# Reordering one head's step on four engines, and splitting a product, in the first attention of a four-stage kernel

## The chip, the cores and the metric

The kernel runs on one core of a Trainium2 chip. The core has a matrix engine (TensorE, PE in the rows; PEld is its weight load), a vector engine (VectorE, DVE), a scalar engine (ScalarE, ACT), GpSimd (POOL) and SyncE (SP), which here only starts transfers. The metric is the device time of one launch in microseconds. Of the kernel before there are three runs: 1880.74, 1884.63 and 1884.85 us, median 1884.63 us.

## The reference, cut to what matters

The input x is 8 x 512 x 128. It passes four blocks, each of the form `x = layernorm(x + block(x))`. The change is in the first one, an attention with 16 heads of 8 channels in which each score also has two terms that depend on the clipped distance of query and key:

```
Q, K, V = heads(x @ Wq.T + bq), heads(x @ Wk.T + bk), heads(x @ Wv.T + bv)      # 8 batches x 16 heads, 512 x 8
rel_pos = clip(k - q + 64, 0, 127);  p2c_pos = clip(q - k + 64, 0, 127)
scores  = Q @ K.T * scale
c2p     = take_along(Q @ pos_key.T * scale, rel_pos)
p2c     = take_along(K @ pos_query.T * scale, p2c_pos).T
probs   = softmax(scores + c2p + p2c)
ctx     = probs @ V;   out = ctx @ Wo.T + bo
```

The other blocks are a gated feed-forward layer, a second attention of 16 heads, and a ternary feed-forward layer. Everything is in float32.

## The kernel before, in words

The 8 x 16 = 128 heads of the first attention (`attention(0)`, where `rel` is true) are worked off one after the other. One head is one *step*; each engine has its own function for a step (`shifted_tensor_step`, `shifted_vector_step`, `shifted_scalar_step`, `sync_step`), and these functions write the order of the engine's instructions out by hand. Four steps are unrolled ahead of a loop, the loop holds 8 steps, and the rest follows it. The engines meet only through semaphores. In a step of head h:

- The 512 x 512 scores are four tiles of 128 queries. **S** (`score_tile`, L821, L823, L827) makes a tile in a PSUM bank, S0 to S3 for the tiles 6 to 9 ahead of the head's first. Its last matmul (L827) writes one spare block into `bank[4]`, which all tiles share, so it waits until VectorE has used the spare block of the tile before (`fixed`).
- **M** (`mix`, L934) on VectorE copies that spare block into the tile under a mask, **F** (`finish`, L946) adds the band of distance terms, and **X** (`row_max`, L954) takes the negated row maximum. M and F of a step work on the tiles that S made; X on the tile one earlier (X0 to X3: 5 to 8 ahead). F needs the band, and X needs F of its tile.
- **E** (`exp_tile`, L1044) on ScalarE exponentiates, E0 to E3 for the tiles 4 to 7 ahead. E3 therefore follows X2, and it is the last tile of head h+1.
- **T** (`turn`, L842) transposes one column block k of the head's own probabilities by four matmuls, and **CT** (`copy_turned`, L1051) on ScalarE copies it to SBUF. T0 of the next step waits for E3 and CT3 of this one; T2 waits for CT1, T1 for the correction's copy (CO, L761), and T3 for KO.
- **W** (`weigh`, L855) multiplies the probabilities of the *previous* four heads (a group, `GROUP` = 4) with their values: step j of a group adds column block j % 4 of all four heads, in four float32 matmuls of 32 output rows each, one per head, side by side in the array. After the last of the four steps ScalarE copies the group's result out (**GO**, `group_out`, L1057), and SyncE stores it (L671) and then loads new values (L673).
- **K** (`key_side`, L741) makes a distance table of the keys for the head 7 ahead, in a bank that CT0 must have emptied; VectorE copies it out (**KO**, L755). SyncE writes it to `shear_a` (L634), waits until it has landed, and reads it back skewed (L640, `a_sheared`). **C** (`correction`, L748 and L749) of the head 5 ahead needs this; ScalarE copies it out (CO, L761), and SyncE writes it to `shear_b` (L646) and reads the skewed band (L652).
- SyncE also loads the operands of the head 8 ahead (`head_load`, L608, L609), and once in a group a table and offsets (L621 to L629). Its queue is in order, so each `hold` (a wait) stops all that is behind it.

Of the kernel before, what the change touches and what calls it, by code (L numbers as in the profile page):

```python
# [21 lines left out]
B, T, C = 8, 512, 128  # L22
# [23 lines left out]
GROUP = 4  # L46
# [4 lines left out]
CORR_AHEAD, KEY_AHEAD, LOAD_AHEAD = 5, 7, 8  # L51
# [13 lines left out]
def build(nc, t):  # L65

    top = ExitStack()
    with top:
# [430 lines left out]
        def attention(layer):  # L499
# [175 lines left out]
            def sync_step(sp, i, j, left, weighed=True):  # L675

                n = unroll * i + j
                if rel:
                    if left >= CORR_AHEAD + 1:
                        shear_a_write(sp, Head(i, j + CORR_AHEAD + 1))  # L680
                    if left >= LOAD_AHEAD:
                        hold(sp, score_mm, 4 * (n + 1))
                        head_load(sp, Head(i, j + LOAD_AHEAD))
# [3 lines left out]
                    if left >= CORR_AHEAD - 2:  # L687
                        shear_b_read(sp, Head(i, j + CORR_AHEAD - 2))
                    if j % GROUP == GROUP - 1 and left >= LOAD_AHEAD + GROUP:
                        tab_load(sp, Head(i, j + LOAD_AHEAD + 1))  # L690
# [98 lines left out]
            def program(block, before, after):  # L789
# [79 lines left out]
                def shifted_tensor_step(pe, i, j, left, weighed=True):  # L869
# [4 lines left out]
                    turn(pe, own, 1)  # L874
                    if left >= KEY_AHEAD:
                        pe.wait_ge(copied, BASE + 4 * own.n + 1)
                        key_side(pe, Head(i, j + KEY_AHEAD), key_bank)
                    if weighed:
                        weigh(pe, Head(i, j - j % GROUP - GROUP), j % GROUP, slice(0, T))
                    turn(pe, own, 2)  # L880
                    score_ahead_of(pe, i, j, left, 2)
                    turn(pe, own, 3)
                    score_ahead_of(pe, i, j, left, 3)
# [84 lines left out]
                def _(v):  # L968
# [26 lines left out]
                    def shifted_vector_step(i, j, left, weighed=True):  # L995
                        mix_ahead_of(i, j, left, 0)
                        max_ahead_of(i, j, left, 0)
                        mix_ahead_of(i, j, left, 1)
                        finish_ahead_of(i, j, left, 0)
                        finish_ahead_of(i, j, left, 1)  # L1000
                        max_ahead_of(i, j, left, 1)
                        if left >= KEY_AHEAD:
                            key_out(v, Head(i, j + KEY_AHEAD), key_bank)
                        max_ahead_of(i, j, left, 2)
                        mix_ahead_of(i, j, left, 2)
# [54 lines left out]
                def _(act):  # L1060
# [8 lines left out]
                    def shifted_scalar_step(i, j, left, weighed=True):  # L1069
                        own = Head(i, j)  # L1070
                        copy_turned(act, own, 0)
                        exp_ahead_of(i, j, left, 0)
# [3 lines left out]
                        copy_turned(act, own, 2)  # L1076
                        exp_ahead_of(i, j, left, 3)
                        copy_turned(act, own, 3)
                        if weighed and j % GROUP == GROUP - 1:
                            group_out(act, Head(i, j - j % GROUP - GROUP))  # L1080
# [1041 lines left out]
```

## Time and profile before

| | |
|---|---|
| profiled execution | 1880.74 us, span 1879.0 us |
| median of three runs | 1884.63 us |
| PE busy | 1699.8 us, 90% |
| DVE busy | 1468.3 us, 78% |
| ACT busy | 1448.4 us, 77% |
| transfers | 404.45 MB, 69.3% of 16 engines' time |

One execution is profiled, so times inside the program are compared with 1879.0 us and not with the median. Busy shares are means over four blocks with different limits; the first attention takes about the stretch from 180 to 830 us, in which PE, DVE and ACT are all near nine or ten tenths busy. PE's matmuls overlap in the pipeline, so its busy share is not the share of its peak. What follows is read from start to start of instructions in this stretch.

### The profile page before, as it was taken

The page shows a single profiled execution, that of the slowest core. Times are in us where ns is not written, and L with a number is a line of the kernel's source. Part 1 is how long each engine was busy: PE and PEld are TensorE (multiplying, and loading weights), DVE is VectorE, ACT ScalarE, POOL GpSimd, SP SyncE. Part 2 cuts the span into 40 slices and gives each one's busy share as a digit, 9 for nine tenths or more (in the row PEclk, how much of TensorE's full clock was granted, in tenths as well). Part 3 has the DMA queues.
Part 4 walks back from the last instruction along what each step waited for, and adds up shares of the span by engine and source line. Part 5 has one row for each costly group of instructions (what it writes and reads, how often), then busy time and mean ns, then how long its engine had stood idle before and what let it go on. Part 6 is the DMA issues. An engine that isn't in the chain of part 4 may idle for free.

```text
span 1879.0 us, 44062 instructions
## 1 busy us (share of the span) xinstructions
PE 1699.8 (90%) x11694; PEld 1033.3 (55%) x11694; DVE 1468.3 (78%) x3533; ACT 1448.4 (77%) x2573; POOL 80.2 (4%) x102
## 2 busy tenths in 40 slices
PE   5369999999999999878758999999999989999998
PEld 2146666666666666545535666666666544455453
DVE  5659999999999999859887999999999873443332
ACT  4449999998999999859888999999999972322222
POOL 0000000000000000015410000000000000000000
PEclk9669999999999999989879999999999999999999
DMA  6778999998999999766998777777777751010000
GB/s 195 273 245 274 300 292 307 298 297 278 288 289 295 297 287 301 234 190 231 344 333 241 220 221 217 223 219 217 222 221 213 224 155 40 28 39 22 22 6 12
DMA packets 414360, 404.45 MB, mean 215 GB/s; under 512 B 36969, under 2 KB 334561, under 8 KB 414177
## 3 DMA queue, kind: packets, MB, share of 16 engines
q1 hardware_dynamic: 414305, 403.80, 69.3%
q8 instruction: 24, 0.39, 0.1%
q14 instruction: 31, 0.25, 0.0%
HBM read 226.89 MB, written 176.30 MB: 215 GB/s over the span
## 4 chain that ended last, share of the span: by engine, by line
PE 54%; DMA 14%; SPq 9%; issue 7%; DVE 7%; ACT 6%; DVEq 0%; POOL 0%; ACTq 0%; POOLq 0%
PE bank L842 15%; PE bank L1934 12%; PE bank L855 8%; DMA a_band<-shear_e 5%; PE bank L821 5%; DMA shear_a<-a_keyside 4%; PE bank L748 3%; DMA a_sheared<-shear_a 2%; DVE a_negmax L954 2%; PE bank L823 2%; ACT a_probt L1051 2%; PE bank L1926 1%; PE bank L1927 1%; PE bank L827 1%; PE bank L1955 1%
## 5 line engine op out<-in xcount | busy, mean ns | idle before, releaser
L1044 ACT ACTIVATE a_prob<-bank,a_negmax 128x512 f32<-128x512 f32 x1024 | 702.6, 741 | 27.4 <-DVE a_negmax L954 25.8
L954 DVE TENSOR_REDUCE a_negmax<-bank 128x1 f32<-128x512 f32 x1024 | 695.1, 679 | 0.2 <-issue 0.2
L1051 ACT COPY a_probt<-bank 128x512 f32<-128x512 f32 x1024 | 599.4, 633 | 28.0 <-PE bank L842 23.5
L842 PE MATMUL bank<-ident,a_prob 128*128 128x128 f32 x4096 | 602.6, 281 | 13.1 <-ACT a_probt L1051 9.7
L842 PEld LDWEIGHTS bank<-ident,a_prob 128*128 128x128 f32 x4096 | 446.4, 142 | 170.9 <-ACT a_probt L1051 117.3
L946 DVE TENSOR_TENSOR bank<-bank,a_band 128x128 f32<-128x128 f32 (+3 forms) x1024 | 339.1, 343 | 71.9 <-DMA a_band<-shear_e 24.4
L821 PE MATMUL bank<-a_stks 74*128 74x192 bf16 (+7 forms) x1024 | 324.7, 317 | 29.7 <-ACT a_prob L1044 26.0
L855 PE MATMUL bank<-a_probt,a_vs 128*32 128x512 f32 x2048 | 274.8, 611 | 0.8 <-ACT a_probt L1051 0.4
L823 PE MATMUL bank<-a_stks 74*128 74x320 bf16 (+5 forms) x768 | 201.3, 262 | 0.0
L821 PEld LDWEIGHTS bank<-a_stks 74*128 74x128 bf16 (+1 forms) x1024 | 100.5, 98 | 163.8 <-ACT a_prob L1044 143.6
L934 DVE COPY_PREDICATED bank<-a_mask,bank 128x128 f32<-128x128 uint32 (+1 forms) x512 | 140.2, 274 | 20.1 <-PE bank L827 18.6
L748 PE MATMUL bank<-ident,a_sheared 128*128 128x128 f32 x512 | 110.3, 293 | 33.2 <-DMA a_sheared<-shear_a 25.8
L2000 DVE TENSOR_TENSOR d_drop<-bank,d_s 128x128 f32<-128x128 f32 x32 | 7.1, 283 | 170.4 <-PE bank L1955 170.4
L827 PE MATMUL bank<-a_stks 74*128 74x128 bf16 (+1 forms) x512 | 112.0, 219 | 6.2 <-DVE bank L934 5.8
L761 ACT COPY a_corr<-bank 128x512 f32<-128x512 f32 x128 | 76.2, 595 | 51.8 <-PE bank L749 38.6
L1934 PE MATMUL bank<-d_ha,d_h1T 128*128 128x512 f32 x256 | 112.3, 592 | 0.0
L1934 PE MATMUL bank<-d_hb,d_h2T 128*128 128x512 f32 x256 | 111.2, 592 | 0.0
L755 DVE COPY a_keyside<-bank 128x512 f32<-128x512 f32 x128 | 86.7, 678 | 19.8 <-PE bank L741 19.8
L748 PEld LDWEIGHTS bank<-ident,a_sheared 128*128 128x128 f32 x512 | 74.8, 146 | 46.5 <-issue 25.1
L749 PE MATMUL bank<-a_tabs,a_stks 65*128 65x128 bf16 x512 | 98.6, 226 | 0.0
L1985 ACT ACTIVATE d_hb<-bank,d_fs 128x512 f32<-128x512 f32 x32 | 22.0, 688 | 90.6 <-PE bank L1934 90.6
L827 PEld LDWEIGHTS bank<-a_stks 74*128 74x128 bf16 x512 | 49.3, 96 | 73.3 <-DVE bank L934 47.9
(179 smaller groups left out, 1597.5 us busy)
## 6 DMA issues: line engine op xcount, KB each, us to landing
a_band<-shear_b SPq DMA_DIRECT2D x128, 512.0 KB, 5.2
shear_a<-a_keyside SPq DMA_DIRECT2D x128, 256.0 KB, 4.1
a_sheared<-shear_a SPq DMA_DIRECT2D x128, 256.0 KB, 4.1
shear_b<-a_corr SPq DMA_DIRECT2D x128, 256.0 KB, 3.4
shear_e<-a_corr SPq DMA_DIRECT2D x128, 256.0 KB, 2.3
a_band<-shear_e SPq DMA_DIRECT2D x128, 256.0 KB, 3.3
a_stks<-stack SPq DMA_DIRECT2D x256, 96.0 KB, 2.5
a_stks<-stack SPq DMA_DIRECT2D x384, 48.0 KB, 2.4
```

Of the source, the lines that this page charges most:

```text
L748: pe.matmul(corr_bank[:, q], sheared[h.slot % 4][:, q], ident[:, :], is_transpose=True, start=True, stop=False)
L821: last = pe.matmul(score[:, 0:c], k[:, qlo, q], k[:, keys, 0:c], start=True, stop=True)
L823: last = pe.matmul(score[:, c:T], k[:, qhi, q], k[:, keys, c:T], start=True, stop=True)
L827: last = pe.matmul(other[:, 0:e - a], k[:, qhi, q], k[:, keys, a:e], start=True, stop=True)
L842: last = pe.transpose(turned_bank[k][:, n * 128:(n + 1) * 128], prob[h.slot % 2][:, n, k * 128:(k + 1) * 128], ident[:, :])
L855: part = pe.matmul(cbank[32 * j:32 * j + VW, cols], vs[g][:, at:at + VW], probt[h.slot + j][:, k, cols], start=(k == 0), stop=(k == NT - 1 ...
L934: v.copy_predicated(score[:, a:e], mask[:, 0:e - a], other[:, 0:e - a]).then_inc(fixed, 1)
L946: v.tensor_tensor(score[:, a:e], score[:, a:e], band[h.slot % bands][:, n, w:w + e - a], ALU.add).then_inc(added, 1)
L954: v.tensor_reduce(negmax[h.slot % 2][:, n:n + 1], score[:, :], AX.X, ALU.max, negate=True).then_inc(maxed, 1)
L1044: nc.scalar.activation(prob[h.slot % 2][:, n, :], score[:, :], ACT.Exp, bias=negmax[h.slot % 2][:, n:n + 1]).then_inc(exped, 1)
L1051: nc.scalar.copy(probt[h.slot][:, k, :], turned_bank[k][:, :]).then_inc(copied, 1)
L1934: last = pe.matmul(dst[:, :], w[:, k, 128 * m:128 * m + 128], src[:, k, :], start=(k == 0), stop=(k == KH - 1))
```

## The change

On PE, W moves from behind K to ahead of it, S2 moves from behind T2 to ahead of it, and in three of four steps W is cut into two halves of 256 columns, the second behind T2. On VectorE, each F comes after an X, so that M and F of one tile no longer stand side by side. On ScalarE, E0 moves ahead of CT0, and GO moves from behind CT3 to ahead of E3. On SyncE the operand load moves behind the two `shear_b` transfers, and waits for the row maxima of the head in place of its scores.

```diff
@@ sync_step
-                    if left >= LOAD_AHEAD:
-                        hold(sp, score_mm, 4 * (n + 1))
-                        head_load(sp, Head(i, j + LOAD_AHEAD))
                     if left >= CORR_AHEAD - 1:
                         hold(sp, added, 4 * (n + 1))
                         shear_b_write(sp, Head(i, j + CORR_AHEAD - 1))
                     if left >= CORR_AHEAD - 2:
                         shear_b_read(sp, Head(i, j + CORR_AHEAD - 2))
+                    if left >= LOAD_AHEAD:
+                        hold(sp, maxed, 4 * (n + 1))
+                        head_load(sp, Head(i, j + LOAD_AHEAD))
@@ shifted_tensor_step
                     turn(pe, own, 1)
+                    if weighed:
+                        weigh(pe, Head(i, j - j % GROUP - GROUP), j % GROUP, slice(0, T // 2 if j % GROUP else T))
                     if left >= KEY_AHEAD:
                         pe.wait_ge(copied, BASE + 4 * own.n + 1)
                         key_side(pe, Head(i, j + KEY_AHEAD), key_bank)
-                    if weighed:
-                        weigh(pe, Head(i, j - j % GROUP - GROUP), j % GROUP, slice(0, T))
+                    score_ahead_of(pe, i, j, left, 2)
                     turn(pe, own, 2)
-                    score_ahead_of(pe, i, j, left, 2)
+                    if weighed and j % GROUP:
+                        weigh(pe, Head(i, j - j % GROUP - GROUP), j % GROUP, slice(T // 2, T))
+                    score_ahead_of(pe, i, j, left, 3)
                     turn(pe, own, 3)
-                    score_ahead_of(pe, i, j, left, 3)
@@ shifted_vector_step
                         max_ahead_of(i, j, left, 0)
+                        finish_ahead_of(i, j, left, 0)
                         mix_ahead_of(i, j, left, 1)
-                        finish_ahead_of(i, j, left, 0)
+                        max_ahead_of(i, j, left, 1)
                         finish_ahead_of(i, j, left, 1)
-                        max_ahead_of(i, j, left, 1)
                         if left >= KEY_AHEAD:
                             key_out(v, Head(i, j + KEY_AHEAD), key_bank)
+                        mix_ahead_of(i, j, left, 2)
                         max_ahead_of(i, j, left, 2)
-                        mix_ahead_of(i, j, left, 2)
                         finish_ahead_of(i, j, left, 2)
@@ shifted_scalar_step
+                        exp_ahead_of(i, j, left, 0)
                         copy_turned(act, own, 0)
-                        exp_ahead_of(i, j, left, 0)
                         copy_turned(act, own, 1)
                         exp_ahead_of(i, j, left, 1)
                         exp_ahead_of(i, j, left, 2)
                         copy_turned(act, own, 2)
+                        if weighed and j % GROUP == GROUP - 1:
+                            group_out(act, Head(i, j - j % GROUP - GROUP))
                         exp_ahead_of(i, j, left, 3)
                         copy_turned(act, own, 3)
-                        if weighed and j % GROUP == GROUP - 1:
-                            group_out(act, Head(i, j - j % GROUP - GROUP))
```

PE before, in one step of a loop turn: T1 (L842), K (L741), the four matmuls of W (L855), T2, and S2 (L821 to L827).

```order
L842 MATMUL bank<-ident,a_prob_52 128x128 x4
L739 ISA
L740 ISA
L741 MATMUL bank<-a_stks,a_tabs 128x512
L855 MATMUL bank<-a_probt_57,a_vs_62 32x512
L855 MATMUL bank<-a_probt_58,a_vs_62 32x512
L855 MATMUL bank<-a_probt_59,a_vs_62 32x512
L855 MATMUL bank<-a_probt_60,a_vs_62 32x512
L842 MATMUL bank<-ident,a_prob_52 128x128 x4
L820 ISA
L821 MATMUL bank<-a_stks 128x192
L823 MATMUL bank<-a_stks 128x320
```

PE now, the same place: T1, the first half of W, K, S2, T2, and the start of the second half.

```order
L842 MATMUL bank<-ident,a_prob_52 128x128 x4
L855 MATMUL bank<-a_probt_57,a_vs_62 32x256
L855 MATMUL bank<-a_probt_58,a_vs_62 32x256
L855 MATMUL bank<-a_probt_59,a_vs_62 32x256
L855 MATMUL bank<-a_probt_60,a_vs_62 32x256
L739 ISA
L740 ISA
L741 MATMUL bank<-a_stks,a_tabs 128x512
L820 ISA
L821 MATMUL bank<-a_stks 128x192
L823 MATMUL bank<-a_stks 128x320
L825 REGISTER_ALU
```

W stood between K and T2 in one piece; now K stands behind W, and S2 and T2 stand between the halves.

VectorE before, from KO (L755) over X2 (L954), M2 (L934), F2 (L946), M3 and X3 to F3.

```order
L755 COPY a_keyside_73<-bank 128x512
L954 TENSOR_REDUCE a_negmax_63<-bank 128x1
L931 ISA
L934 COPY_PREDICATED bank<-a_mask,bank 128x128
L946 TENSOR_TENSOR bank<-bank,a_band_71 128x192
L931 REGISTER_ALU
L934 COPY_PREDICATED bank<-a_mask,bank 128x128
L953 REGISTER_ALU
L954 TENSOR_REDUCE a_negmax_64<-bank 128x1
L946 TENSOR_TENSOR bank<-bank,a_band_71 128x256
```

VectorE now, the same place (its lines are two further down in the file).

```order
L755 COPY a_keyside_73<-bank 128x512
L933 ISA
L936 COPY_PREDICATED bank<-a_mask,bank 128x128
L956 TENSOR_REDUCE a_negmax_63<-bank 128x1
L948 TENSOR_TENSOR bank<-bank,a_band_71 128x192
L933 REGISTER_ALU
L936 COPY_PREDICATED bank<-a_mask,bank 128x128
L955 REGISTER_ALU
L956 TENSOR_REDUCE a_negmax_64<-bank 128x1
L948 TENSOR_TENSOR bank<-bank,a_band_71 128x256
```

X2 has moved in between M2 and F2; KO stays ahead of both.

## Rows read from the trace of the kernel before

**Rows 1.** The page's costliest groups: line, engine, op | busy, mean ns | idle before.

```profile
L842 PE MATMUL bank<-ident,a_prob 128*128 128x128 f32 x4096 | 602.6, 281 | 13.1 <-ACT a_probt L1051 9.7
L855 PE MATMUL bank<-a_probt,a_vs 128*32 128x512 f32 x2048 | 274.8, 611 | 0.8 <-ACT a_probt L1051 0.4
```

**Rows 2.** Busy us of each engine from 200 to 700 us; then clock, DMA share, GB/s.

```profile
200.00:700.00 500.00, 488.65 (x4087) 316.10 (x4085) 476.01 (x1208) 470.37 (x860) 0.00 (x0) 1.00 0.93 293
```

**Rows 3.** Groups by line from 200 to 700 us: C's transposes and their waits.

```profile
L748 PE MATMUL bank<-ident,a_sheared 128*128 128x128 f32 x372 | 77.2, 285 | 9.5 <-DMA a_sheared<-shear_a 7.0 <-ACT a_probt L1051 2.3
```

**Rows 4.** Timeline of DVE: start us, length us, engine, line; one step.

```profile
501.01 0.28 DVE L934 COPY_PREDICATED bank<-a_mask,bank 128x128 f32<-128x128 uint32 x1
...
501.81 0.22 DVE L934 COPY_PREDICATED bank<-a_mask,bank 128x64 f32<-128x64 uint32 x1
501.94 0.69 DVE L946 TENSOR_TENSOR bank<-bank,a_band 128x256 f32<-128x256 f32 x2
...
503.13 0.68 DVE L755 COPY a_keyside<-bank 128x512 f32<-128x512 f32 x1
503.73 0.68 DVE L954 TENSOR_REDUCE a_negmax<-bank 128x1 f32<-128x512 f32 x1
504.33 0.28 DVE L934 COPY_PREDICATED bank<-a_mask,bank 128x128 f32<-128x128 uint32 x1
504.73 0.37 DVE L946 TENSOR_TENSOR bank<-bank,a_band 128x192 f32<-128x192 f32 x1
505.06 0.30 DVE L934 COPY_PREDICATED bank<-a_mask,bank 128x128 f32<-128x128 uint32 x1
505.26 0.68 DVE L954 TENSOR_REDUCE a_negmax<-bank 128x1 f32<-128x512 f32 x1
...
506.19 0.29 DVE L934 COPY_PREDICATED bank<-a_mask,bank 128x128 f32<-128x128 uint32 x1
```

**Rows 5.** Timeline of PE, one step, first matmul of each block.

```profile
500.61 0.63 PE L842 MATMUL bank<-ident,a_prob 128*128 128x128 f32 x4
...
501.07 0.38 PE L821 MATMUL bank<-a_stks 74*128 74x512 bf16 x1
...
501.44 0.65 PE L842 MATMUL bank<-ident,a_prob 128*128 128x128 f32 x4
501.93 0.38 PE L741 MATMUL bank<-a_stks,a_tabs 65*128 65x512 bf16 x1
502.24 1.06 PE L855 MATMUL bank<-a_probt,a_vs 128*32 128x512 f32 x8
503.23 0.66 PE L842 MATMUL bank<-ident,a_prob 128*128 128x128 f32 x4
503.73 0.25 PE L821 MATMUL bank<-a_stks 74*128 74x192 bf16 x1
...
504.00 0.61 PE L842 MATMUL bank<-ident,a_prob 128*128 128x128 f32 x4
...
504.77 0.30 PE L748 MATMUL bank<-ident,a_sheared 128*128 128x128 f32 x1
...
505.78 0.63 PE L842 MATMUL bank<-ident,a_prob 128*128 128x128 f32 x4
```

**Rows 6.** Timeline of PEld, the weight load behind W.

```profile
503.23 0.42 PEld L842 LDWEIGHTS bank<-ident,a_prob 128*128 128x128 f32 x4 [0.84 <-ACT a_probt L1051]
```

**Rows 7.** Timeline of ACT: E3, CT3, and GO of the next step.

```profile
504.44 0.71 ACT L1044 ACTIVATE a_prob<-bank,a_negmax 128x512 f32<-128x512 f32 x1
505.03 0.60 ACT L1051 COPY a_probt<-bank 128x512 f32<-128x512 f32 x1
...
510.68 0.61 ACT L1057 COPY a_outs<-bank 128x512 f32<-128x512 f32 x1
```

**Rows 8.** Timeline of SP's queue: the skewed read, and the group's store.

```profile
510.50 0.35 SPq L640 DMA_DIRECT2D a_sheared<-shear_a  x1
511.55 0.38 SPq L671 DMA_DIRECT2D heads_out<-a_outs  x1
```

## The prediction

> **What bounds the kernel now.** I read the busy shares first, then the timelines of one undisturbed step engine by engine, then the groups by line, for who waits. From 200 to 700 us PE, DVE and ACT are busy for 489, 476 and 470 of 500 us at the full clock (1.00, that is 2.4 GHz), and the transfers take 0.93 of the 16 DMA engines' time [rows 2]. So everything is nearly full, and the busy shares name no bound. C's four transposes per head number 372, so 93 heads pass in these 500 us, 5.38 us each [rows 3]. An undisturbed step is shorter: VectorE starts M0 at 501.01 and the next M0 at 506.19, 5.18 us, and no row in between shows an idle gap [rows 4]. PE's step from T0 to T0 is 5.17 us, but S1 to T1 takes 0.37 us where S2 to T3 takes 0.27 for more columns: 0.10 is a wait for VectorE [rows 5]. VectorE sets an undisturbed step. The other 0.20 us per head are disturbances; about half of it is C, which waits for its skewed read: 9.5 us in 500 [rows 3], 0.10 per head.
>
> The change touches some 30 groups of four heads. That is the unit of the sum: 0.1 us per group is 3 us.
>
> **VectorE.** M2 to F2 takes 0.40 us, and F2 to M3 0.33, where M3 to X3 takes 0.20 [rows 4]: F2 needs M2, which is 0.28 long, so it starts 0.12 behind M2's end. With X2 in between, M2 takes 0.20, and F2 0.27 (F0 and F1 together take 0.59: 1.19 from F0 to KO less one X of 0.60 [rows 4]). That saves 0.26. Against it, X1 now stands only one M1 (0.13) behind the F0 that it needs. A shorter F is 0.37 long; with the same 0.12 that is 0.49 at least against 0.33 + 0.13 = 0.46, and for F0's 256 columns I take 0.07 of new wait; X3 has 0.02 of the same kind. With the rest kept VectorE's own step is 5.18 - 0.26 + 0.09, about 5.02.
>
> **PE: what W costs in two halves.** One matmul of 512 columns is recorded with 0.611 us, one of 128 with 0.281 [rows 1], both float32: 0.86 ns per column. W's x8 are two ranks of four side by side, so 2 x 512 x 0.86 = 0.88 of its 0.99 us [rows 5] are columns and 0.11 is fixed. Half a W is then 0.44 + 0.11 = 0.55. The bounds of this unseen block are 0.50 (half of 0.99, all of it columns) and 0.99 (none of it); I take 0.55, since the column rate comes from rows. Ahead of W stands a gap: K is 0.13 longer than S2's first matmul for 320 more columns, so its 512 columns take 0.21, but W starts 0.31 behind it [rows 5]: 0.10. The load behind W starts with T2 itself at 503.23, after PEld idled for 0.84 us [rows 6]: weights are not brought in while W runs, at either edge.
>
> With T = 0.46 (T0 to S1), S = 0.27, K = 0.21, S3 and T3 together 0.73 and C with S0 1.01 (C to T0) [rows 5], and the gap of 0.10 ahead of each W, a step with halves, counted from T0, has S1 at 0.46, T1 0.73, W 1.29, K 1.84, S2 2.05, T2 2.32, the second half 2.88, S3 3.43, T3 3.70, C 4.16, and the next T0 at 5.17. A step with a whole W has K at 2.28 and PE would be through at 4.96. PE is therefore the new limit of the three split steps, at 5.17, against VectorE's 5.02: what VectorE gains is hidden behind it.
>
> **A wait that comes in with the whole W.** In one step of four K stands behind a whole W: it starts at 2.28, not at 1.32 as now (501.93 - 500.61). It is 0.38 long, so KO starts at about 2.72; M2 stands behind KO at 3.32, and X2 at 3.52. Behind that stand others: X2 ends and E3 starts 0.71 behind X2's start (503.73 to 504.44 [rows 4, 7]), CT3 0.59 later, and CT3 is 0.60 long [rows 7], with some 0.05 to PE. T0 of the next step needs both: 3.52 + 0.71 + 0.59 + 0.65 = 5.47. In the kernel before the same chain has 1 us to spare.
>
> **ScalarE.** E0 ahead of CT0 uses the time in which ScalarE waits for T0; K and T2 need CT0 and CT1, and in the new order reach them 0.5 us later than now, so this costs nothing as long as K stays behind W. GO ahead of E3 has a price: the second half of W starts at 2.88 and drains by 2.88 + 0.55 + 0.07 (1.06 less 0.99 [rows 5]) = 3.50; GO at 3.53, E3 half a us behind it at 4.03, CT3 4.62, next T0 5.27. It occurs once in a group.
>
> Sum of a group: 5.47 + 5.27 + 2 x 5.17 = 21.08 against 4 x 5.18 = 20.72, so +0.36, times 30: +11 us.
>
> **SyncE and the transfers.** The chain behind C's waits starts at GO: it starts at 510.68 and is 0.61 long, the store is issued at 511.55 [rows 7, 8], and the shear_a write, its landing and the skewed read for a C two steps later stand behind the store. GO comes at 3.53 instead of 4.90 (510.68 less 505.78), but the skewed read of its own step is issued only at 510.50 and each issue takes about half a us, so the store can move from 511.55 to about 511.05 at most. Besides, PE's and ScalarE's longer step leaves the transfers 0.36 us more per group. C's waits are 9.5 x 30 x 21.5 / 500, about 12 us over the stage (21.5 is four heads of 5.38). I take three quarters of it as gone, -9 us; the bounds are 0 and -12. The operand load moved behind the shear_b transfers costs nothing: it fills the time until shear_a has landed, and its new condition, X2 of the step before, is older than the write ahead of it. In the group's last step the shear_b write may now stand and wait for CO for a few tenths, in front of the loads; that is in the 0 to -12.
>
> Net: +11 - 9 = +2 us. From the profiled 1880.74 that is 1883; from the median, 1884.63, it is 1887, and I name 1886.
>
> **Rule of the Trainium skill against the rows.** The rows show no weight load under a running W [rows 6]. The Trainium skill, TensorE: Matmul & The Clock Gate, section Part 2, says that the engine's reorder window pulls weight loads ahead of matmuls in flight when row groups do not conflict or the background buffer is free. By that rule neither edge of W would cost anything, and halving it would be nearly free; that is the first rival below. The trace speaks against it.
>
> **The rivals.**
> - *The edges of W are hidden once it stands between other blocks.* For it: K and S2 bring bfloat16 weights, unlike T2, whose load is the one that the rows show late. Against it: the 0.10 between K and W is such an edge, and it is not hidden. Without gaps (0.10 ahead and 0.11 fixed, per block) a split step is 4.75 on PE, so VectorE limits it to 5.02; the whole-W chain is 5.47 - 0.21 = 5.26. Group 5.26 + 3 x 5.02 = 20.32, -0.40, times 30 = -12, with C's waits -9 more: 1864.
> - *The halves cost more than their columns.* PE is then the bound through six halves per group. Each 0.01 us on a half is 0.06 per group, 1.8 us in all. At 0.65 (0.10 over mine, well inside the bound of 0.99) a split step is 5.37, and the sum +2 + 18 = +20: 1905. For it: each half loads its four weights anew. Against it: no row shows a fixed part above 0.11. It decides from 0.57 on, where the loss passes 0.3%.
> - *The transfers bound it.* 0.93 x 5.38 = 5.00 us of the DMA engines per head; nothing below 5.0 can be had, and near it landing times grow. It takes away a faster PE's gain and leaves 1885.
>
> That the order does not change is excluded: the four functions write it out.
>
> **Numbers.** Forecast (no change that shows) 0.38, with the transfer case in it; its own range is 1879 to 1890. Hidden edges, and cases between, 0.28; costly halves, or C's waits unrelieved with the +11 in full (1896), 0.34. About 0.3%, 5.7 us, is what a measurement tells from no change. Faster 0.29, same 0.37, slower 0.34. The range reaches most of the way to both rivals: 1866 to 1904.
>
> **What would show it.** In the new profile: VectorE without the 0.40 behind M2, but with idle time again; half a W at 0.55 from its start to the next block; in one step of four KO released by K and the next T0 late by 0.3; GO about 3.5 us behind T0; the wait at L748 well under 9.5 us in the same stretch. I am wrong if the undisturbed group is under 20.5 us, or if a half takes 0.60 or more.

## The result, and the profile after

The changed kernel takes 1936.22 us (median of four runs, 1933.13 to 1944.24) against 1884.68 us for the kernel before on the same chip: ratio 1.0285, 95% interval 1.0251 to 1.032. It is slower by 52 us. I had forecast 1886 us and a range that ended at 1904. The profiled execution took 1944.98 us, with a span of 1943.2.

Busy time of each engine from 200 to 700 us after, with the clock, the DMA share and GB/s at the end. It answers to [rows 2].

```profile
200.00:700.00 500.00, 461.63 (x4243) 307.87 (x4245) 430.52 (x1103) 432.57 (x783) 0.00 (x0) 0.97 0.88 268
```

All three engines have lost 27 to 46 us of work in the same 500 us, and the transfers have dropped from 0.93 to 0.88. So neither an engine nor the transfers became the bound: everybody waits. The clock is no longer fully granted either (0.97). The groups by line of the same stretch (busy us, mean ns, then idle us ahead and who ended it) say who is waited for; the first answers to [rows 3].

```profile
L748 PE MATMUL bank<-ident,a_sheared 128*128 128x128 f32 x340 | 71.3, 287 | 0.0
...
L755 DVE COPY a_keyside<-bank 128x512 f32<-128x512 f32 x85 | 58.4, 687 | 47.4 <-PE bank L741 47.4
...
L741 PE MATMUL bank<-a_stks,a_tabs 65*128 65x512 bf16 x84 | 32.6, 388 | 30.1 <-DMA a_stks<-stack 20.3 <-issue 7.7 <-ACT a_probt L1053 1.9
```

KO (L755) numbers 85, so a head takes 5.88 us instead of 5.38. C's wait is gone, from 9.5 us to nothing, as forecast in number; whether for the reason that I gave is taken up behind the experiments. In its place K (L741) waits for its operands, a wait that the kernel before does not have. The list of waits shows two more places (us in total, times, longest); the first row is K's weight load, the other two are SyncE's own queue.

```profile
PEld bank L741 <- issue: 43.6, 28, 2.8
...
SPq L598 <- ACT a_corr L761: 85.4, 54, 3.4
SPq L598 <- DMA shear_a<-a_keyside: 31.9, 22, 2.3
```

SyncE's waits of the kernel before, in the same view:

```profile
SPq L598 <- DMA shear_a<-a_keyside: 68.8, 63, 3.8
...
SPq L598 <- ACT a_corr L761: 1.6, 1, 1.6
```

It waited for `shear_a` to land, 18 times for GO (12.0 us, none of it left now), and once for CO. Now it stands 54 times in the `hold` for CO, with the operand load queued behind. One such place in full: PE and ACT first (start us, length, engine, line, idle time ahead in brackets), then SyncE's queue.

```profile
502.14 0.64 PE L855 MATMUL bank<-a_probt,a_vs 128*32 128x256 f32 x8
504.77 0.39 PE L741 MATMUL bank<-a_stks,a_tabs 65*128 65x512 bf16 x1 [1.99 <-DMA a_stks<-stack]
...
505.29 0.61 PE L842 MATMUL bank<-ident,a_prob 128*128 128x128 f32 x4
...
507.00 1.06 PE L842 MATMUL bank<-ident,a_prob 128*128 128x128 f32 x4
...
509.47 0.59 ACT L761 COPY a_corr<-bank 128x512 f32<-128x512 f32 x1 [0.78 <-PE bank L749]
```

```profile
497.35 0.37 SPq L646 DMA_DIRECT2D shear_b<-a_corr  x1
497.84 0.58 SPq L652 DMA_DIRECT2D a_band<-shear_b  x1
498.84 0.34 SPq L608 DMA_DIRECT2D a_stks<-stack  x1
499.37 0.35 SPq L609 DMA_DIRECT2D a_stks<-stack  x1
...
510.14 0.37 SPq L646 DMA_DIRECT2D shear_b<-a_corr  x1
```

K is ready to start behind the half W, at about 502.8, and starts at 504.77. The load that it needs was issued at 499.37, 2.0 us behind the `shear_b` write, and behind the 512 KB band read, with only its own first part (L608) between. As PE works in order, T, C and CO come late with it, and the next `shear_b` write is only issued at 510.14. The stop costs more than its 2 us: this step takes 8.79 us from T0 (500.87) to T0 (509.66). Two windows of 6 us around it (same columns as above):

```profile
500.00:506.00 6.00, 3.83 (x39) 2.47 (x40) 3.75 (x10) 4.07 (x9) 0.00 (x0) 1.00 1.00 315
506.00:512.00 6.00, 6.00 (x48) 3.94 (x41) 4.33 (x13) 4.32 (x8) 0.00 (x0) 0.72 0.62 182
```

After PE has been idle for 2 us the granted clock falls to 0.72 in the next window; from 507 to 509 us it is 0.50, the 1.2 GHz level. There T's four matmuls take 1.06 us instead of 0.61.

### The profile page after: what moved, and what is told of

It reads as the page before. It is cut to its first block, busy times and chain, and to the rows that moved or that the text cites. A ratio compares the mean times of both kernels' runs of the same rounds, so it can differ in the third digit from the quotient of the medians.

```text
span 1943.2 us, 45550 instructions
## 1 busy us (share of the span) xinstructions
PE 1721.4 (89%) x12438; PEld 1057.7 (54%) x12438; DVE 1463.4 (75%) x3533; ACT 1453.5 (75%) x2573; POOL 80.1 (4%) x102
## 4 chain that ended last, share of the span: by engine, by line
PE 43%; SPq 16%; issue 13%; DMA 12%; DVE 8%; ACT 7%; DVEq 0%; POOL 0%; ACTq 0%; POOLq 0%
PE bank L1936 11%; PE bank L842 10%; PE bank L855 6%; DMA a_band<-shear_e 6%; DMA a_stks<-stack 4%; PE bank L821 4%; DVE a_negmax L956 3%; ACT a_probt L1053 3%; ACT a_prob L1046 2%; PE bank L823 2%; PE bank L1928 1%; PE bank L1929 1%; DVE bank L948 1%; PE bank L741 1%; PE bank L748 1%
## 5 line engine op out<-in xcount | busy, mean ns | idle before, releaser
L1053 ACT COPY a_probt<-bank 128x512 f32<-128x512 f32 x1024 | 584.9, 624 | 71.7 <-PE bank L842 70.8
L842 PE MATMUL bank<-ident,a_prob 128*128 128x128 f32 x4096 | 603.8, 281 | 21.8 <-ACT a_probt L1053 15.5
L842 PEld LDWEIGHTS bank<-ident,a_prob 128*128 128x128 f32 x4096 | 451.8, 143 | 89.9 <-issue 51.3
L948 DVE TENSOR_TENSOR bank<-bank,a_band 128x128 f32<-128x128 f32 (+3 forms) x1024 | 350.4, 342 | 58.8 <-DMA a_band<-shear_e 29.0
L821 PE MATMUL bank<-a_stks 74*128 74x192 bf16 (+7 forms) x1024 | 328.1, 321 | 33.9 <-ACT a_prob L1046 30.6
L855 PE MATMUL bank<-a_probt,a_vs 128*32 128x256 f32 (+1 forms) x2792 | 298.1, 501 | 0.4 <-ACT a_probt L1053 0.4
L821 PEld LDWEIGHTS bank<-a_stks 74*128 74x128 bf16 (+1 forms) x1024 | 100.6, 98 | 218.7 <-ACT a_prob L1046 176.8
L755 DVE COPY a_keyside<-bank 128x512 f32<-128x512 f32 x128 | 87.9, 687 | 83.0 <-PE bank L741 82.8
L748 PE MATMUL bank<-ident,a_sheared 128*128 128x128 f32 x512 | 109.7, 292 | 25.3 <-DMA a_sheared<-shear_a 20.3
L827 PE MATMUL bank<-a_stks 74*128 74x128 bf16 (+1 forms) x512 | 111.2, 217 | 5.9 <-DVE bank L936 4.8
L741 PE MATMUL bank<-a_stks,a_tabs 65*128 65x512 bf16 x128 | 51.3, 400 | 58.1 <-DMA a_stks<-stack 25.9
L855 PEld LDWEIGHTS bank<-a_probt,a_vs 128*32 128x32 f32 x2792 | 56.3, 109 | 68.2 <-issue 68.0
```

The costliest lines, as they stand in the source:

```text
L748: pe.matmul(corr_bank[:, q], sheared[h.slot % 4][:, q], ident[:, :], is_transpose=True, start=True, stop=False)
L821: last = pe.matmul(score[:, 0:c], k[:, qlo, q], k[:, keys, 0:c], start=True, stop=True)
L827: last = pe.matmul(other[:, 0:e - a], k[:, qhi, q], k[:, keys, a:e], start=True, stop=True)
L842: last = pe.transpose(turned_bank[k][:, n * 128:(n + 1) * 128], prob[h.slot % 2][:, n, k * 128:(k + 1) * 128], ident[:, :])
L855: part = pe.matmul(cbank[32 * j:32 * j + VW, cols], vs[g][:, at:at + VW], probt[h.slot + j][:, k, cols], start=(k == 0), stop=(k == NT - 1 ...
L948: v.tensor_tensor(score[:, a:e], score[:, a:e], band[h.slot % bands][:, n, w:w + e - a], ALU.add).then_inc(added, 1)
```

## The experiments

Ratios are to the kernel before on the same chip, with the 95% interval. All waits are sums over 200 to 700 us. The notation "e1 +" means that a kernel starts from e1, which is the changed kernel with SyncE's old order.

**Which engine's order costs the time?** First SyncE: once taken back, once put alone into the kernel before.

```diff
@@ sync_step (e1: the changed kernel; e2 is the kernel before with the reverse edit)
+                    if left >= LOAD_AHEAD:
+                        hold(sp, score_mm, 4 * (n + 1))
+                        head_load(sp, Head(i, j + LOAD_AHEAD))
                     ...shear_b_write, shear_b_read
-                    if left >= LOAD_AHEAD:
-                        hold(sp, maxed, 4 * (n + 1))
-                        head_load(sp, Head(i, j + LOAD_AHEAD))
```

> The changed kernel with SyncE's old order (operand load first, released by the scores). Theory A: the load of the head 8 ahead now stands behind the shear_b write, which waits for the correction's copy, so it lands too late for K one step later (67 waits for that copy, 105 us, and PE's K waiting 20 us for a load by name, 84 us in all, from 200 to 700 us); with the old order K waits for no load and the time is 1875 to 1892 us. Theory B: the orders on PE, VectorE and ScalarE (halved W, K behind W) are the loss; then it stays at 1920 or more. An even split would read about 1910.

> The kernel before with SyncE's new order alone. Theory A: most of the loss is here, 1920 to 1945 us, with PE waiting at L741 for the operand load. Theory B: no change, 1880 to 1890. A rival within A: in the old PE order K comes early in the step (1.3 us behind T0 instead of 1.8 or 2.3), so a late load hurts more here than in the changed kernel, over 1945.

Measured: e1 0.9967 (0.9942 to 0.9993), e2 1.0428 (1.0384 to 1.0472). e2's median is 1973 us, over the 1920 to 1945 of theory A, as its rival with the earlier K had it. (The 67 waits and 105 us for CO in the first expectation belong to a stretch that reaches beyond 700 us; up to there they are the 54 and 85.4 above.) The whole loss is SyncE's, and it needs nothing of the other three edits; the three together save some 0.3%. K's waits in e1, then in e2:

```profile
DVE a_keyside L755 <- PE bank L741: 14.8, 46, 0.5
PEld bank L741 <- issue: 14.2, 23, 0.8
```

```profile
PEld bank L741 <- issue: 36.6, 21, 3.5
...
PE bank L741 <- DMA a_stks<-stack: 29.1, 11, 3.3
```

The 14.2 us of e1 come once in four steps (x23), with no transfer late: K's weights stand behind the whole W. Only what exceeds it I count as a load that is late. The profile names no releaser for these waits, so this is inferred from how they come and go with the load's place: they are 14.2 again in e3 and e13. It makes 29 us in the changed kernel, which with the 28 us of the PE row (20.3 and 7.7) makes 57. KO's wait says the same: 47.4 against 14.8.

**Is it the place of the load, or its new condition?** e3 has the new condition in the old place.

```diff
@@ sync_step (e1 +)
-                        hold(sp, score_mm, 4 * (n + 1))
+                        hold(sp, maxed, 4 * (n + 1))
```

> The changed kernel with the operand load back in its old place, but with the new condition (row maxima instead of scores). Theory A says the place is what costs, not the condition: within 0.5% of the kernel with SyncE's old order. If the condition costs, it lies with the changed kernel at about 1935.

Measured 0.9977 (0.9957 to 0.9997), and K waits for no load. It is the place.

**Which place?** Three other ones. A `shear_a` write opens SyncE's step, `shear_b` write and read follow, the skewed read of `shear_a` closes it.

```diff
@@ sync_step: order of the transfers
 before, e1     shear_a write, LOAD, shear_b write, band read, shear_a read
 after          shear_a write, shear_b write, band read, LOAD, shear_a read
+e5             shear_a write, shear_b write, LOAD, band read, shear_a read
+e12            shear_a write, shear_b write, band read, shear_a read, LOAD
+e13            LOAD, shear_a write, shear_b write, band read, shear_a read
```

> The changed kernel with the operand load between the shear_b write and the shear_b read: still behind the wait for the correction's copy, but one issue (about 0.5 us) and one wait earlier. If what costs is the wait for the copy ahead of the load, most of the loss stays: ratio to the kernel before 1.018 to 1.03 (changed kernel 1.0285). If it is the amount of transfers put ahead (a 512 KB band read among them), it falls to 1.00 to 1.012.

> The changed kernel with the operand load still further back, behind the skewed read of shear_a, which waits until the write of shear_a has landed (3.8 us). Loss theory: load, K, C, the correction's copy and the shear_b write that waits for it form a loop over two steps, in which every us ahead of the load adds 0.5 us per step. The load is issued 1 to 2 us later, so 0.5 to 1 us per step over 124 steps, 60 to 120 us on top of the changed kernel: ratio 1.06 to 1.095. If the loss came from the shear_b transfers being early, and not from the load being late, it stays near 1.03.

> SyncE's old order, but with the operand load at the head of the step, ahead of the shear_a write; the changed orders elsewhere. Theory: with the load ahead of the shear_b write K waits for no load any more, so an earlier load gains nothing: 0.997 as with the old order. If the shear_a write, its landing and the skewed read are what limits a disturbed step, a later shear_a write (by two issues, 1 us) shows as a loss, 1.003 to 1.01.

Measured: e5 1.0005 (0.9985 to 1.0025), e12 1.013 (1.01 to 1.0159), e13 0.9975 (0.996 to 0.9991). e5 also stands behind the wait for CO and costs nearly nothing. e12 is a miss: the load is issued later than in the changed kernel and yet only about half as much is lost. How late the load is issued does not by itself set the price, so my theory at that point fell. What differs is the time that the second load (L609) takes to land. For the kernels before, after, e5 and e12, in this order (us, minimum, median, maximum), and last for e14, which comes below:

```profile
DMA to landing us min/median/max: 1.8/3.1/6.0
```

```profile
DMA to landing us min/median/max: 3.0/4.3/5.7
```

```profile
DMA to landing us min/median/max: 2.1/3.8/5.1
```

```profile
DMA to landing us min/median/max: 2.0/2.9/4.1
```

```profile
DMA to landing us min/median/max: 2.6/3.8/5.1
```

**Wait for CO ahead, 512 KB ahead, or both?** e14 and e15 move the band read to the front; e16 leaves the new order as it is and fetches half of the band, e17 does this under the old order. In e16 and e17 half of each band row keeps old values, so the correction is computed from partly old numbers.

```diff
@@ sync_step: order of the transfers
+e14            shear_a write, band read, LOAD, shear_b write, shear_a read
+e15            shear_a write, band read, shear_b write, LOAD, shear_a read
@@ shear_b_read (e16: the changed kernel, e17: e1)
-                [[PITCH_B - 1, 128], [1, NT * wide]]
+                [[PITCH_B - 1, 128], [1, NT * wide // 2]]
```

> The changed kernel with SyncE's order band read, operand load, shear_b write: the load is directly behind the 512 KB read, as in the change, but no longer behind the write that waits for CO. Theory A (the load is late only when its issue, which stands behind CO, and its landing behind the 512 KB read add up past K's turn): it is issued some 2 us earlier, so a longer landing (4.0 to 4.6 us for the second load, 4.3 in the change) costs nothing; ratio 0.994 to 1.004, K waits for no load. Rival C (the 512 KB read directly ahead is enough by itself): 1.01 to 1.03 and K waits for loads 15 times or more in 500 us. Rival B (only the place behind CO counts): 0.997, like SyncE's old order, so it does not part from A here.

> The changed kernel with SyncE's order band read, shear_b write, operand load: against the change only the band read moves, from between write and load to ahead of the write, so the load stands behind the wait for CO as before, 0.5 us of issuing earlier, and behind 256 KB more recent transfers instead of 512. Theory A: landing of the second load 3.3 to 3.9 us (4.3 in the change), its issue 0.5 us earlier, margin 0.9 to 1.5 us larger; ratio 1.000 to 1.008, K's waits for the load under 20 us in 500. Rival B (the place behind CO is the price): 1.02 to 1.03, waits of 50 us or more. Rival C: 0.997 to 1.003.

> The changed kernel with SyncE's new order untouched; the band read fetches the first half of each row alone in the looped steps (256 KB instead of 512 KB; the other half of the band holds old values, so the scores' correction is computed from old numbers). Theory A: the load is issued at the same place behind CO, but lands behind 256 KB: second load 3.2 to 3.8 us instead of 4.3; ratio to the kernel before 0.990 to 1.004, K's waits for loads under 20 us in 500. Rival B (place behind CO): 1.015 to 1.03. To be read against the same halving under SyncE's old order.

> The same halving of the band read (256 KB of 512, the correction is computed from partly old numbers) with SyncE's old order and the changed orders of the three engines. 0.985 to 0.998: what 256 KB less a head give where no load is late. Theory A: within 0.5 per cent of the halved read under the new order. Rival B: 1.5 per cent or more faster than that. If transfers bounded this kernel, 15 per cent fewer bytes would bring it under 0.95.

Measured: e14 1.0482 (1.0453 to 1.0511), e15 1.0414 (1.039 to 1.0439). Both expectations failed, and neither kernel tests what it was made for: moved to the front, the band read meets its own write. SyncE's waits and a piece of its queue in e14:

```profile
SPq L598 <- DMA shear_b<-a_corr: 142.1, 60, 3.5
```

```profile
504.93 0.32 SPq L652 DMA_DIRECT2D a_band<-shear_b  x1
...
506.33 0.35 SPq L609 DMA_DIRECT2D a_stks<-stack  x1
506.87 0.39 SPq L646 DMA_DIRECT2D shear_b<-a_corr  x1
...
511.33 0.32 SPq L652 DMA_DIRECT2D a_band<-shear_b  x1
```

The band read of 511.33 waits for the write of 506.87 to land; in every order but these two the wait for CO of the following step lay between the two and hid it. SyncE's queue is now itself the loop that sets the step, 6.4 us long here. I had overlooked this wait when I wrote what to expect. One thing can still be read from e14: behind the 512 KB read, but ahead of the write, the second load lands after 3.8 us at the median, as it does in e5 behind the write alone. Behind both, in the changed kernel, it takes 4.3.

e16 and e17 do decide: e16 0.9988 (0.9975 to 1.0), e17 0.9945 (0.9921 to 0.997). With 256 KB less in front of it, the load in its bad place costs 0.4%, not 3.2% (1.0285 against 0.9967). SyncE's waits in e16, K's wait for the load, and the landing of L609:

```profile
SPq L598 <- ACT a_corr L762: 68.1, 59, 1.6
```

```profile
PE bank L742 <- DMA a_stks<-stack: 0.3, 1, 0.3
```

```profile
DMA to landing us min/median/max: 2.3/3.2/3.6
```

SyncE still waits for CO in 59 places, so the load is issued just as late; it lands 1.1 us sooner at the median and 2.1 us sooner at worst, and K no longer waits. The table puts this together for an undisturbed step. The write (L646) starts about 0.6 us behind T0 (0.7 in e2), L609 so much later as the second column says, and K of the next step is due 7.1 us behind T0 (5.21 + 1.85, and some hundredths; 6.5 in e2, which has PE's old order, 5.17 + 1.32). What is left for the landing is the third column. The fifth counts the landings that took longer than that.

| | L609 behind L646 | left for the landing | landing, median and longest | landings over what is left | K waits for loads | ratio |
|---|---|---|---|---|---|---|
| e16 | 1.94 | 4.6 | 3.2, 3.6 | 0 of 92 | 1 | 0.9988 |
| e5 | 1.36 | 5.1 | 3.8, 5.1 | 0 of 92 | 2 | 1.0005 |
| e12 | 3.39 | 3.1 | 2.9, 4.1 | 14 of 90 | 22 | 1.013 |
| after | 1.93 | 4.6 | 4.3, 5.7 | 30 of 84 | 57 | 1.0285 |
| e2 | 1.94 | 3.9 | 4.0, 5.7 | 45 of 81 | 62 | 1.0428 |

(Medians over 200 to 700 us; K's waits are PE's for the load and for issue at L741 plus its weight load's for issue, less the 14.2 of e1, or the 7.2 of the kernel before in e2.) In e16 and after, the same time is left, and only the landing differs: this pair shows that the late landing is what costs. In e12 the load has the least time left and still less is lost than in the changed kernel: half as many of its landings come too late. The count moves with the time left (with 0.1 us less it is 22 and 36 for e12 and after), the order of the five kernels does not.

e16 does not show that it is the place of the read alone that makes the landing long, since it also moves fewer bytes in all (a DMA share of 0.82 against 0.88). Four kernels with the same orders on the engines part the two: under SyncE's old order the median landing is 3.2 us with the whole read (e1) and 2.6 with half of it (e17), under the new order 4.3 (after) and 3.2 (e16). So 256 KB less per head shorten the landing by 0.6 us even where the load stands ahead of the read, and the place behind the two `shear_b` transfers adds 1.1 us with the whole read and 0.6 with half of it.

**What each other edit does.** PE's order alone, VectorE's alone, both without ScalarE's; SyncE's order is the old one in all three.

```diff
@@ the kernel before, with these functions taken from the changed kernel
+e4             shifted_tensor_step
+e9             shifted_vector_step
+e10            shifted_tensor_step, shifted_vector_step
```

> The kernel before with PE's new order alone (W ahead of K, halves, S2 ahead of T2). By the sum of the prediction PE's split steps take 5.17 us and the step with a whole W 5.47, on VectorE's old 5.18: theory A gives 1885 to 1900 us. Theory B gives 1910 or more.

> The kernel before with VectorE's new order alone. VectorE's own work falls to 5.02 us a step, so by that alone it is the fastest, ratio 0.985 or less. But M2 now stands ahead of X2, and in PE's old order S2, which M2 waits for, comes only behind K, W and T2, 3.1 us behind T0: S2's last matmul 3.3, M2 3.6, X2 3.8, E3 4.5, CT3 5.1, next T0 5.75. The chain theory says slower: undisturbed steps of about 5.7 us, ratio 1.04 to 1.07.

> The kernel before with the new orders on PE and VectorE, ScalarE and SyncE as before. PE's order alone gave 1.0137 (steps of 5.53 and 6.0 us). If the orders on PE and VectorE belong together and ScalarE's is a side matter, steps are 5.2 and 5.5 to 5.7, and the ratio lies with SyncE's old order alone (0.9967), 0.995 to 1.000. If ScalarE's E0 ahead of CT0 is needed, it stays above 1.005.

Measured: e4 1.0137 (1.0092 to 1.0183), e9 1.037 (1.0343 to 1.0397, just under what was expected), e10 1.0016 (0.9999 to 1.0034, just over the 0.995 to 1.000 expected). e4 is a miss: 1917 us where the sum of the prediction gave 1885 to 1900. The longest waits of e4, then of e9 (27.4 and 8.6 us in the kernel before):

```profile
PEld bank L827 <- DVE bank L936: 67.2, 177, 1.1
```

```profile
DVE bank L934 <- PE bank L827: 80.7, 83, 1.2
```

Each order alone waits for the other engine, through the spare block that all score tiles share. Only as a pair do they come out even; with ScalarE's they give the 0.3% of e1; e10 and e1 differ by no more than the edge of their intervals.

Then the three choices inside the new orders: K ahead of the whole W (e6), GO behind CT3 as before (e7), the whole W in every step (e8).

```diff
@@ shifted_tensor_step (e1 +, e6)
-                    if weighed:
-                        weigh(pe, ..., slice(0, T // 2 if j % GROUP else T))
+                    if weighed and j % GROUP:
+                        weigh(pe, ..., slice(0, T // 2))
                         key_side(pe, Head(i, j + KEY_AHEAD), key_bank)
+                    if weighed and j % GROUP == 0:
+                        weigh(pe, ..., slice(0, T))
@@ shifted_scalar_step (e1 +, e7)
-                        group_out ahead of exp_ahead_of(i, j, left, 3)
+                        group_out behind copy_turned(act, own, 3)
@@ shifted_tensor_step (e1 +, e8)
-                        weigh(pe, ..., slice(0, T // 2 if j % GROUP else T))
+                        weigh(pe, ..., slice(0, T))
                     ...
-                    if weighed and j % GROUP:
-                        weigh(pe, ..., slice(T // 2, T))
```

> SyncE's old order, the changed orders elsewhere, and K ahead of the whole W in the one step of four that has it. With SyncE's old order undisturbed steps take 5.21 us with halves and 5.77 with a whole W (group 21.42). If KO behind K behind the whole W makes the 5.77, this step falls to about 5.2 and the group to 20.85, 0.57 less: some 17 us, ratio to before about 0.988. If it is the W itself on PE, the step stays at 5.6 or more, and the ratio at 0.996. Transfers near their limit could give part of it back: 0.992.

> SyncE's old order, the changed orders elsewhere, but the group's copy (GO) behind CT3 as in the kernel before. The prediction held that the earlier GO relieves C's wait for its skewed read by up to 12 us in the stage: then this is slower than SyncE's old order alone (0.9967) by 0.3 to 0.6%, 1.000 to 1.003, and SyncE waits for GO at the store again. If the longer step on PE gave the relief, it stays at 0.997.

> SyncE's old order, the changed orders elsewhere, but W whole in every step, ahead of K. If the chain K, KO, X2, E3, CT3 behind a whole W sets a step at 5.77, all four take it: group 23.1 against 21.42, +1.65, times 30 is +50 us, ratio 1.022 (less where disturbed steps hide it: 1.012 and up). If PE's work per step rules, two blocks less per step make it faster than 0.9967.

Measured: e6 0.9984 (0.9958 to 1.0009), e7 0.9985 (0.9966 to 1.0005), e8 1.0075 (1.005 to 1.01). e6 (expected 0.988) and e8 (expected 1.012 to 1.022) are misses: both were reckoned from a whole-W step of 5.77 us and three of 5.21, but e1's group is one of 5.53 (whole W), one of 5.46 (GO) and two of 5.21. In e6 it takes 5.61: KO now comes early, but M2 stands idle for 0.50 us until PE has made S2's spare block, which the whole W ahead of S2 delays as much as it delayed K, and X2, E3 and CT3 follow as before. Four undisturbed steps take 21.49, 21.36 and 22.41 us, against 21.42 in e1. So the halves do pay, 0.25 us a step (22.41 less 21.42, over four), with the rest of the order as it is. Where K stands in the one whole-W step and where GO stands is worth nothing that can be told from e1 (e7's ratio lies between the two that were expected and decides nothing). For GO, e7's waits say the same, C's for its skewed read and SyncE's for GO at the store:

```profile
PE bank L748 <- DMA a_sheared<-shear_a: 3.1, 6, 1.0
```

```profile
SPq L598 <- ACT a_outs L1059: 18.4, 20, 1.5
```

With GO late SyncE waits for it again, as it does in the kernel before (12.0 us), and C still waits no longer than in e1 (3.1 against 5.5 us).

No version that computes the whole correction is clearly better than e1, e3 and e13, which lie 0.2 to 0.3% under the kernel before.

## Why the prediction was wrong

**The step that failed** is on SyncE: "The operand load moved behind the shear_b transfers costs nothing: it fills the time until shear_a has landed, and its new condition is older than the write ahead of it." I compared the load with the two conditions at its front and never with who needs it behind, which is K of the next step. Three things were missed. Without the load in front (two issues of 0.5 us) SyncE reaches the `shear_b` write before CO is done: 85.4 us of waits where I wrote "a few tenths" in one step of four (68.1 in e16, where no load is late, so most of it does not come from a late K). Behind the write stand 2 us of issuing, up to L609. And the load's landing, which I took as given, grows from a median of 3.1 to 4.3 us behind the 256 KB write and the 512 KB read. With 4.6 us left for it, 30 of 84 landings are too late. e1 and e2 show that this is the whole loss, e3 that the condition is innocent, e16 that with a shorter landing nearly all of it goes, though SyncE waits for CO 59 times; e5 shows that the wait for CO alone does no harm.

On this the Trainium skill, DMA: Bandwidth & Descriptors, section Queues, rings and completion order, says that each DMA engine consumes the descriptors of a queue in ring order. The landings fit this, as far as they can show it: in the changed kernel, behind the write and the read, none is under 3.0 us, in e14, behind the read alone, none under 2.6, while 1.8 us occurs in the kernel before. An order of descriptors is not seen in any row here, and fewer bytes in all shorten the landing too.

**The schedule of PE** was right. One undisturbed step of e1, whose order on PE is that of the changed kernel:

```profile
502.39 0.63 PE L842 MATMUL bank<-ident,a_prob 128*128 128x128 f32 x4
502.85 0.38 PE L821 MATMUL bank<-a_stks 74*128 74x512 bf16 x1
...
503.10 0.64 PE L842 MATMUL bank<-ident,a_prob 128*128 128x128 f32 x4
503.67 0.64 PE L855 MATMUL bank<-a_probt,a_vs 128*32 128x256 f32 x8
504.24 0.39 PE L741 MATMUL bank<-a_stks,a_tabs 65*128 65x512 bf16 x1
...
504.74 0.60 PE L842 MATMUL bank<-ident,a_prob 128*128 128x128 f32 x4
505.28 0.64 PE L855 MATMUL bank<-a_probt,a_vs 128*32 128x256 f32 x8
505.85 0.31 PE L821 MATMUL bank<-a_stks 74*128 74x320 bf16 x1
...
507.60 0.63 PE L842 MATMUL bank<-ident,a_prob 128*128 128x128 f32 x4
```

From T0 it has T1 at 0.71 (forecast 0.73), W 1.28 (1.29), K 1.85 (1.84), T2 2.35 (2.32), the second half 2.89 (2.88), S3 3.46 (3.43), and the next T0 at 5.21 (5.17). A half of W costs 0.57 us; I had 0.55, and 0.57 is where the rival of costly halves was to set in; by its own rate, 1.8 us for 0.01, this adds 4 us. The rival of hidden edges is refuted by the rows: 0.57 for 256 columns where 512 take 1.00. What the prediction drew from the rule that it weighed (the Trainium skill, TensorE: Matmul & The Clock Gate, Part 2) is not seen either: both edges of W are still paid, since 256 columns are 0.44 of the 0.57. One reading of mine was too strong: of the 0.84 us ahead of T2's weight load [rows 6] PEld waits 0.54 for CT1, whose copy starts at 502.34 and ends at 502.93; only the last 0.30 are a load held back by W.

**VectorE**, in the same step, M2, X2, F2 and M3, and M0 of the next:

```profile
505.38 0.28 DVE L936 COPY_PREDICATED bank<-a_mask,bank 128x128 f32<-128x128 uint32 x1
505.58 0.68 DVE L956 TENSOR_REDUCE a_negmax<-bank 128x1 f32<-128x512 f32 x1
506.18 0.36 DVE L948 TENSOR_TENSOR bank<-bank,a_band 128x192 f32<-128x192 f32 x1
506.45 0.29 DVE L936 COPY_PREDICATED bank<-a_mask,bank 128x128 f32<-128x128 uint32 x1
...
507.86 0.30 DVE L936 COPY_PREDICATED bank<-a_mask,bank 128x128 f32<-128x128 uint32 x1 [0.18 <-PE bank L827]
```

M2 now takes 0.20 and F2 0.27, as forecast to the hundredth, and M0 stands 0.18 us idle for PE: VectorE got faster and waits. The 0.07 of new wait that I took between F0 and X1 did not come: X1 starts 0.46 behind F0 (503.45 to 503.91), 0.04 behind F0's end, so the 0.12 between M2 and F2 is no fixed price of reading what the instruction before wrote.

**The whole-W step** came out at 5.53 us (forecast 5.47), by the chain that I had written down: in the step of e1 whose T0 is at 207.52, KO starts 2.70 us behind T0 (forecast 2.72), M2 3.31 (3.32), X2 3.50 (3.52), E3 4.22 and CT3 4.81, and the next T0 0.72 behind CT3, not 0.65. e6 shows that K is not the only way to this length: with K early the same chain starts at S2. **The GO step** was 5.46 where I had 5.27. Its rows on ScalarE, in a step whose T0 is at 507.60 and the next at 513.06:

```profile
511.27 0.58 ACT L1059 COPY a_outs<-bank 128x512 f32<-128x512 f32 x1
511.75 0.69 ACT L1046 ACTIVATE a_prob<-bank,a_negmax 128x512 f32<-128x512 f32 x1
512.33 0.59 ACT L1053 COPY a_probt<-bank 128x512 f32<-128x512 f32 x1
```

GO starts at 3.67, not 3.53, CT3 at 4.73, not 4.62, and T0 0.73 behind it, not 0.65. Undisturbed groups of e1 take 21.3 to 21.6 us (forecast 21.08) against 20.96 to 21.07 before (I had 20.72): about +0.44, not +0.36, so +13 us over 30 groups.

**C's waits.** I took 9 of 12 us as gone, by an earlier GO and a longer step. In e1 C still waits 5.5 us for its skewed read, where [rows 3] have 9.5 in all, and VectorE's wait for the band, which I had not looked at, goes from 4.3 to 1.1; in the changed kernel C's wait is 0.0, but only because K's is ahead of it. The chain from GO, which I gave as the reason, is not what relieves C: e7 has GO back in its old place and C waits no longer than in e1, and in e10, with ScalarE's old order, SyncE waits 21.0 us for GO and C's wait is 0.5 in all. What does relieve it stays open; the longer step that I named beside it is not tested by itself. How large the relief is stays open too: on one chip e1 is 6.5 us ahead of the kernel before (1886.78 against 1893.26), which with the 13 us of longer groups makes about 20, while the two profiled executions, one each and of different chips, have e1 7 us behind (1887.69 against 1880.74), which would make 6. That my 9 lies between is luck. Without SyncE's edit the time would have been inside the range.

**The transfers as a bound:** e17 moves 256 KB less per head, with a DMA share of 0.81 against 0.94 in e1, and the two intervals overlap (0.9945 and 0.9967). The transfers are not the bound; what counts is when one of them lands.

## What to carry to other kernels

When an in-order queue of transfers is reordered, work out for each moved one the time from its new issue to the instruction that needs its data, and compare this with its longest landing in the trace, not with the median (here 4.6 us were left, and the kernel before already had landings of 3.1 at the median and 6.0 at most); count the issues and waits that now stand ahead of it, and the bytes directly ahead. The small transfer with the nearest deadline belongs in front of the large ones. An order that several engines share is to be tested per engine: here PE's alone lost 1.4%, VectorE's alone 3.7%, and together they cost nothing.

## What the runs showed of the hardware

- The landing of a 48 KB load depends on what was issued just ahead on the same queue: median 4.3 us (minimum 3.0) behind a 256 KB write and a 512 KB read, 3.8 (2.1) behind the write alone (e5), 3.8 (2.6) behind the read alone (e14), 3.2 (2.3) behind the write and the read with 256 KB (e16), 3.1 (1.8) in the kernel before. It also depends on the bytes in all: 2.6 us in e17 against 3.2 in e1, at a DMA share of 0.81 against 0.94.
- A stop of 2 us on PE was followed by a window of 6 us with a granted clock of 0.72, 2 us of it at 0.50. So an occasional late load costs more than its wait: the mean clock of the stretch is 0.97 in the changed kernel and 0.93 in e2, but 1.00 in e1.
- Cutting W's moving operand in two halves costs 2 x 0.57 against 1.00 us, 0.07 for each half.
